# A graph network's last layer: edge features copied into step order during the dense pass, one load a group for the weighted pass, and its one-hot tiles shared by ACT and DVE

## The chip, the cores and the metric

One core of one Trainium2 chip. The metric is the device time of the whole program in microseconds, median of three runs. The engines are called PE (matrix products; PEld is its weight load), DVE (vector), ACT (scalar, pointwise functions), POOL (GpSimd) and SP (issues transfers only). The times of the program before are 5190.69 us (5190.12 to 5192.56).

## The reference

Four graph layers on 6250 nodes with 128 features, and 106250 edges sorted by destination. Only the last one is touched:

```python
xl = (x @ Wl + bl).reshape(n, HEADS, C)          # HEADS 4, C 32
xr = (x @ Wr + br).reshape(n, HEADS, C)
ee = (eattr @ We).reshape(-1, HEADS, C)          # eattr: 64 features of an edge, and for loops their mean by destination
msg = xl[src_a] + xr[dst_a] + ee
score = einsum('ehc,hc->eh', leaky_relu(msg, 0.2), att)
smax = segment_max(score, dst_a); ex = exp(score - smax[dst_a])
out = segment_sum(ex / segment_sum(ex)[dst_a] * xl[src_a], dst_a)
```

After it come a norm over the nodes, relu, and a layer norm of the sum with x. The third layer, which stands just ahead, is x + segment_sum(x[src], dst) and a layer norm.

## The kernel before, in words

Nodes stand in 49 tiles of 128. Edges stand in tiles of 128 in their sorted order, and a **step** is one pair of an edge tile and a node tile that its destinations touch. There are 896 steps (SPX), in 224 groups of GS = 4, and one turn of a hardware loop holds NG3 = 8 groups, so there are 28 turns; `turns` (L60) writes the first turn out apart and loops over 27. The table `g.t` holds the edge tile of each step, `g.T` its node tile; both are read into registers by a TENSOR_LOAD. The stages that matter here run one after the other, each in a block of its own that ends when all engines have come to its end.

**Dense pass** (`dense_pass`, L1982). Layer three is done with a dense matrix of edge counts in DRAM (`g.M`). SP loads it in chunks of four node tiles (`load`, L2007, 6.4 MB each, two buffers `matd`), the next chunk of a buffer as soon as PE has done the four tiles that read it (L2021). PE does 49 matmuls for each of the 49 tiles (L2033) into four PSUM banks. DVE adds the sums and does the layer norm (`add` L2070, `norm` L2082); ACT does one square root a tile (L2110) for which DVE waits in `norm`. The last chunk, number 12, has a single tile and is loaded when chunk 10 is done (L2023, L2024).

**Score pass** (`score_pass`, L2246), between the two stages that are changed. It loads the edge features transposed, one step at a time, by four transfers a group on SP (L2331), after a TENSOR_LOAD of the four tile numbers (L2327). It also gathers the rows of xl and keeps them in DRAM in step order (`g.rows`, L2314).

**Weighted pass** (`weighted_pass`, L2566). For each group G, with ring slot c = G mod 4:

- SP loads the four steps' rows of xl, one transfer (L2599). It waits for POOL to be through with group G-4 (`s_val`).
- ACT reads four tile numbers (L2629), waits until PE has done group G-4 (`s_o`, L2631), issues four transfers of edge features into the last 64 columns of `val` (L2633), and copies the weights of the steps into `val` (L2635).
- POOL multiplies rows by weights into `val` (L2616).
- DVE makes the one-hot tile `hot` of the destinations, 128 x 512 (L2675), and adds the products of group G-2 to the running sums `out` (`add`, L2660): a TENSOR_LOAD of four node tile numbers (L2661), and four adds of 128 x 200 (L2668), each waiting for the one before by `s_out`.
- PE multiplies `hot` and `val`, four steps a group (L2649; a matmul in f32 has two records each), into PSUM. There are two pairs of banks, so PE starts group G when the adds of group G-2 are done (`wait(t, s_out, (G - 1) * GS)`, L2647).

In its first turn SP also loads, after the rows of eight groups, xl and xr of all nodes (L2603, 3.2 MB each) and four vectors (L2606) for the stage that follows.

```python
    def add(G, q):
        v.load(regs, g.T[0:1, bass.ds(G * GS, GS)])
        T = [v.snap(r, min_val=0, max_val=NT - 1) for r in regs]
        wait(v, s_o, G + 1)
        for k in range(GS):
            wait(v, s_out, G * GS + k)
            to = g.out[:, bass.ds(T[k] * FX, FX)]
            v.tensor_tensor(to, to, ops[q % 2][k // 2][...], ALU.add).then_inc(s_out, 1)
```

## Time and profile before

| what | value |
|---|---|
| median of 3 runs | 5190.69 us |
| the profiled execution, its own time | 5189.41 us |
| its span (first to last instruction) | 5187.6 us |
| busy in the span: PE / DVE / ACT / POOL | 73% / 65% / 28% / 56% |
| dense pass | from about 2644 to 3070 us |
| score pass | from about 3117 to 4294 us |
| weighted pass | from about 4392 to 5036 us |

All positions are microseconds from the start of the span. Busy shares over the whole span say little here, since each stage has a bound of its own; the stages are read one by one. "Idle before" in a row is the time in which the engine had nothing to do just ahead of that instruction, with the event that ended it; "issue" means that no event of another engine ended it. Rows of DVEq, ACTq and SPq are work of the engines' instruction queues, such as a TENSOR_LOAD into registers or the issue of a transfer.

### The profile page before, as it was taken

Reading aid. Unit: us, or ns where it says so; the run is one execution under the profiler, and the core shown is the slowest. Engines: PE = TensorE matmul, PEld = TensorE weight load, DVE = VectorE, ACT = ScalarE, POOL = GpSimd, SP = SyncE. Lnnn points to the kernel's source line nnn. Section 1 sums busy time; section 2 is a strip of 40 time slices with the busy share of each in tenths; the row PEclk is TensorE's granted clock in tenths of the full one; section 3 lists DMA queues with packets and bytes.
Section 4 is the critical chain, followed back from the end, with each engine's and each line's share of the span. In section 5 each row is a group of like instructions: output and inputs, shape, how many; then the busy total and the mean of one; then the engine's idle time right before and its main releaser. Section 6 shows DMA issues by size and latency. Waiting matters only on the chain. (4 is left out here: it accounts for less than half of the span.)

```text
span 5187.6 us, 87634 instructions
## 1 busy us (share of the span) xinstructions
PE 3774.7 (73%) x17756; PEld 2581.4 (50%) x17757; DVE 3380.9 (65%) x10123; ACT 1428.3 (28%) x3423; POOL 2918.1 (56%) x2917
## 2 busy tenths in 40 slices
PE   0377777777677777389979988889899883555553
PEld 0266666666434444145546655555555552444442
DVE  5688888888798888343242234445444446788878
ACT  0255555555344434200000012222222221000012
POOL 1477777777367777777400007777777770333334
PEclk9955555665688888689989995555555555999996
DMA  5577777777532232088966636666666663655540
GB/s 104 154 249 250 248 247 248 247 249 254 164 97 87 87 92 91 10 183 199 180 182 205 204 113 171 177 174 179 174 176 177 175 168 59 174 143 142 143 106 25
DMA packets 1057791, 843.64 MB, mean 163 GB/s; under 512 B 546821, under 2 KB 952950, under 8 KB 1044160
## 3 DMA queue, kind: packets, MB, share of 16 engines
q1 hardware_dynamic: 785772, 597.52, 39.1%
q0 software_dynamic: 98096, 176.73, 13.3%
q10 hardware_dynamic: 173844, 68.53, 5.5%
q8 instruction: 26, 0.43, 0.0%
q14 instruction: 53, 0.43, 0.0%
HBM read 601.40 MB, written 167.28 MB: 148 GB/s over the span
## 5 line engine op out<-in xcount | busy, mean ns | idle before, releaser
L2303 POOL DMA_INDIRECT ring<-xl_rows,idx x896 | 895.2, 999 | 847.8 <-DVE idx L2382 575.0
L413 POOL DMA_INDIRECT ringa<-x_sign_pos,idxa x880 | 865.3, 983 | 301.6 <-issue 295.5
L965 POOL DMA_INDIRECT edge_counts<-edge_cnt,places x832 | 827.2, 994 | 359.9 <-issue 272.1
L2375 PE MATMUL zps<-We,eaT 64*128 64x128 f32 x1792 | 712.0, 499 | 0.0
L2649 PE MATMUL ops<-val,hot 128*128 128x200 f32 x1792 | 369.1, 350 | 273.5 <-DVE out L2668 243.1
L2373 PE MATMUL zps<-xr,hotT 128*128 x2688 | 455.2, 302 | 145.1 <-ACT hotT L2355 89.8
L2405 DVE TENSOR_TENSOR z<-zps,ring 128x512 f32<-128x512 f32 x224 | 154.9, 691 | 605.1 <-PE zps L2375 510.0
L2375 PEld LDWEIGHTS zps<-We,eaT 64*128 64x128 f32 x1792 | 448.6, 310 | 163.3 <-issue 145.7
L2616 POOL TENSOR_TENSOR val<-rows,val 128x512 f32<-128x512 f32 x224 | 235.0, 1050 | 508.4 <-ACT val L2635 377.6
L498 PE MATMUL sela<-hota,endsa 128*128 128x128 f32 x1760 | 399.3, 398 | 132.1 <-ACT endsa L439 117.6
L1890 PE MATMUL pss<-x3s,mats 128*128 128x385 bf16 x2401 | 403.4, 330 | 100.9 <-DMA mats<-edge_counts 95.9
L2649 PEld LDWEIGHTS ops<-val,hot 128*128 128x128 f32 x1792 | 301.2, 193 | 341.3 <-DVE out L2668 308.0
L2033 PE MATMUL psd<-x3d,matd 128*128 128x384 bf16 x2401 | 391.7, 327 | 35.3 <-DVE x3d L2064 35.3
L498 PEld LDWEIGHTS sela<-hota,endsa 128*128 128x128 f32 x1760 | 342.3, 290 | 149.9 <-issue 102.9
L2373 PEld LDWEIGHTS zps<-xr,hotT 128*128 128x128 bf16 x2688 | 225.3, 121 | 361.6 <-issue 354.9
L2351 ACT ACTIVATE apartT<-dstb,minus_p 128x512 f32<-128x512 f32 x224 | 161.7, 722 | 869.6 <-DMA dstb<-dst_in_tile 866.0
L2668 DVE TENSOR_TENSOR out<-out,ops 128x200 f32 x896 | 321.5, 359 | 115.5 <-PE ops L2649 17.6
L1890 PEld LDWEIGHTS pss<-x3s,mats 128*128 128x128 bf16 x2401 | 235.2, 98 | 269.2 <-DMA mats<-edge_counts 83.8
L1240 DVE SCALAR_TENSOR_TENSOR equalb<-keyb,key_cols,earlier 128x256 f32<-128x256 f32 x850 | 359.9, 481 | 5.9 <-issue 3.3
L506 PE MATMUL msgTa<-ident,msga 128*128 128x128 f32 x880 | 241.2, 428 | 153.3 <-DVE msga L578 150.8
L2033 PEld LDWEIGHTS psd<-x3d,matd 128*128 128x128 bf16 x2401 | 235.3, 98 | 191.7 <-DVE x3d L2064 35.7
L570 DVE TENSOR_TENSOR acc<-acc,sela 128x128 f32 x880 | 251.9, 286 | 117.5 <-issue 16.4
(359 smaller groups left out, 5945.3 us busy)
## 6 DMA issues: line engine op xcount, KB each, us to landing
edge_counts<-zeroa SPq DMA_DIRECT2D x55, 1568.0 KB
matd<-edge_counts SPq DMA_DIRECT2D x12, 6272.0 KB
keyb<-edge_keys SPq DMA_DIRECT2D x50, 1216.0 KB
dstb<-dst_in_tile SPq DMA_DIRECT2D x112, 512.0 KB
xl_of_steps<-ring SPq DMA_DIRECT2D x224, 256.0 KB
rows<-xl_of_steps SPq DMA_DIRECT2D x224, 256.0 KB
reseta<-resets SPq DMA_DIRECT2D x110, 512.0 KB
dstba<-dst_in_tile_bf ACTq DMA_DIRECT2D x112, 256.0 KB
```

The source lines that it names most:

```text
L413: p.indirect_dma_start(out=ring[:, k, :], out_offset=None, in_=table, in_offset=bass.IndirectOffsetOnAxis(ap=idx[:, k:k + 1], axis=0)).the ...
L498: ins = t.matmul(sel[q % 2][:, k * P:(k + 1) * P], ends[:, q % 2, k, :], hot[:, q, k, :], start=True, stop=True)
L570: v.tensor_tensor(to, to, sel[q % 2][:, k * P:(k + 1) * P], ALU.add).then_inc(s_acc, 1)
L965: p.indirect_dma_start(out=g.M.rearrange("d s -> (d s)").unsqueeze(1), out_offset=bass.IndirectOffsetOnAxis(ap=g.place[:, c:c + 1], axis=0 ...
L1240: v.scalar_tensor_tensor(out=equal[:, k % 4, :], in0=keyb[:, i, k * P + HALF:k * P + HALF + WIN], scalar=g.keycol[:, bass.ds(tile, 1)], in ...
L1890: ins = t.matmul(ps[b * WC + k][:, 0:3 * F + 1], mat[:, b, T, k * P:(k + 1) * P], x3[:, T, 0:3 * F + 1], start=T == 0, stop=T == NT - 1)
L2033: ins = t.matmul(ps[k][:, 0:3 * F], mat[:, b, T, k * P:(k + 1) * P], x3[:, T, :, :].rearrange("p i f -> p (i f)"), start=T == 0, stop=T == ...
L2303: p.indirect_dma_start(out=ring[:, c, k, :], out_offset=None, in_=g.xl_rows[0:N, :], in_offset=bass.IndirectOffsetOnAxis(ap=idx[:, q * GS ...
L2373: t.matmul(zk, hotT[:, b, k * P:(k + 1) * P], g.xr3[:, bass.ds(T[k] * (3 * F) + i * F, F)], start=i == 0, stop=False)
L2375: ins = t.matmul(zk, eaT[:, c, k, :], g.We[:, :], start=False, stop=True)
L2649: ins = t.matmul(ops[q % 2][k // 2][:, (k % 2) * FX:(k % 2 + 1) * FX], hot[:, c, k, :], val[:, c, k, :], start=True, stop=True)
L2668: v.tensor_tensor(to, to, ops[q % 2][k // 2][:, (k % 2) * FX:(k % 2 + 1) * FX], ALU.add).then_inc(s_out, 1)
```

## The change

In the dense pass, all 896 steps' edge features (32 KB each) are copied from the input in DRAM to a new tensor `g.ea` in DRAM, in step order. ACT issues eight copies ahead of each tile's square root (392), SP forty after each chunk's load and 24 at the end (504), each four after a TENSOR_LOAD of four tile numbers; SP waits for all of them at the end of the pass. In the weighted pass SP loads the edge features of a group by one transfer, behind the one for the rows and behind a wait for PE's group G-4. Of the eight one-hot tiles of a turn DVE makes numbers 3 and 7 (two groups ahead of need), ACT the six others, as 1 - |n - d| cut at zero: four Abs of 128 x 128, each with its step's destinations as bias, and one Relu of 128 x 512. DVE's adds now follow their own group's number instead of running two behind.

```diff
--- before.py
+++ after.py
@@ -1979,7 +1979,17 @@
                 norm(ch, CH * WC, 0)
 
 
-def dense_pass(nc, g):
+def copy_attributes(e, g, a, regs, at, n, sem):
+
+    for k in range(0, n, GS):
+        e.load(regs, g.t[0:1, bass.ds(at + k, GS)])
+        t = [e.snap(r, min_val=0, max_val=ET - 1) for r in regs]
+        for i in range(GS):
+            e.dma_start(g.ea[bass.ds(at + k + i, 1), :, :].rearrange("o p w -> o (p w)"),
+                        a["ea"][bass.ds(t[i], 1), :, :].rearrange("o p w -> o (p w)")).then_inc(sem, 16)
+
+
+def dense_pass(nc, g, a):
 
 
 
@@ -2001,9 +2011,18 @@
         tmp, z = m.sb("tmpd", [P, WC, F]), m.sb("zd", [P, WC, F])
         st, mv, root = m.sb("std", [P, WC, 6]), m.sb("mvd", [P, WC, 2]), m.sb("rootd", [P, WC])
         s_var, s_root, s_chain, s_go = m.sem("s_vard"), m.sem("s_rootd"), m.sem("s_chaind"), m.sem("s_god")
+        s_copied = m.sem("s_copied")
+        BY_TILE, BY_LOAD = 8, 40
+        REST = SPX - NT * BY_TILE - CH * BY_LOAD
+        assert 0 <= REST <= BY_LOAD and REST % GS == 0
         with nc.Block() as block:
             @block.sync
             def _(s):
+                regs = [s.alloc_register(f"tcs{j}") for j in range(GS)]
+
+                def copies(c, n=BY_LOAD):
+                    copy_attributes(s, g, a, regs, NT * BY_TILE + c * BY_LOAD, n, s_copied)
+
                 def load(c, b, w):
                     s.dma_start(mat[:, b, :, 0:w * P],
                                 g.M[0:NT * P, bass.ds(c * (WC * P), w * P)].rearrange("(t p) s -> p t s", p=P)
@@ -2016,12 +2035,17 @@
                         load(it * 2 + b, b, WC)
                 load(0, 0, WC)
                 load(1, 1, WC)
+                copies(0)
                 with s.Fori(1, PAIRS) as it:
                     for b in range(2):
                         s.wait_ge(s_pe, (it * 2 + b - 1) * WC)
                         load(it * 2 + b, b, WC)
+                        copies(it * 2 + b - 1)
                 s.wait_ge(s_pe, (CH - 1) * WC)
                 load(CH, 0, 1)
+                copies(CH - 1)
+                copies(CH, REST)
+                s.wait_ge(s_copied, 16 * SPX)
 
             @block.tensor
             def _(t):
@@ -2105,7 +2129,10 @@
 
             @block.scalar
             def _(e):
+                regs = [e.alloc_register(f"tca{j}") for j in range(GS)]
+
                 def one(S, i):
+                    copy_attributes(e, g, a, regs, S * BY_TILE, BY_TILE, s_copied)
                     e.wait_ge(s_var, S + 1)
                     e.activation(root[:, i:i + 1], mv[:, i, 1:2], ACT.Sqrt).then_inc(s_root, 1)
 
@@ -2577,8 +2604,20 @@
         ops = [[m.bank(f"ops4{i}{j}") for j in range(2)] for i in range(2)]
         s_ini = m.sem("s_ini4")
         s_r = [m.sem(f"s_r4{i}") for i in range(NG)]
+        apart = m.sb("apart4", [P, 2, GS * P])
         s_ea = [m.sem(f"s_ea4{i}") for i in range(NG)]
-        s_hot = m.sem("s_hot4")
+        s_ap = m.sem("s_ap4")
+        s_hot, s_hotd = m.sem("s_hot4"), m.sem("s_hotd4")
+        EQ = (3, 7)
+        assert NG3 == 8 and NG == 4
+
+        def on_act(it, q):
+
+            return it * (NG3 - len(EQ)) + q - sum(e < q for e in EQ)
+
+        def on_dve(it, q):
+
+            return it * len(EQ) + EQ.index(q)
         s_ex = m.sem("s_ex4")
         s_val = m.sem("s_val4")
         s_o = m.sem("s_o4")
@@ -2598,6 +2637,9 @@
                         wait(s, s_val, G - NG + 1)
                         s.dma_start(rows[:, c, :].rearrange("p (k f) -> p k f", k=GS),
                                     g.rows[bass.ds(G * GS, GS), :, :].rearrange("k e f -> e k f")).then_inc(s_r[c], 16)
+                        wait(s, s_o, G - NG + 1)
+                        s.dma_start(val[:, c, :, F + 2 * HEADS:FX],
+                                    g.ea[bass.ds(G * GS, GS), :, :].rearrange("k e f -> e k f")).then_inc(s_ea[c], 16)
                     if isinstance(it, int):
                         for to, of in ((g.xl, g.xl_rows), (g.xr, g.xr_rows)):
                             s.dma_start(to[:, :].rearrange("p (t f) -> p t f", f=F), of.rearrange("(t p) f -> p t f", p=P)
@@ -2621,19 +2663,24 @@
 
             @block.scalar
             def _(s):
-                regs = [s.alloc_register(f"t4{j}") for j in range(GS)]
-
                 def body(it):
                     for q in range(NG3):
                         G, c = it * NG3 + q, q % NG
-                        s.load(regs, g.t[0:1, bass.ds(G * GS, GS)])
-                        t = [s.snap(r, min_val=0, max_val=ET - 1) for r in regs]
                         wait(s, s_o, G - NG + 1)
-                        for k in range(GS):
-                            s.dma_start(val[:, c, k, F + 2 * HEADS:FX], a["ea"][bass.ds(t[k], 1), :, :].rearrange("o p w -> p (o w)")
-                                        ).then_inc(s_ea[c], 16)
                         s.activation(val[:, c, :, F:F + 2 * HEADS], exm[:, GS * q:GS * (q + 1), :, bass.ds(it, 1)].rearrange("p c k o -> p c (k o)"),
                                      ACT.Copy).then_inc(s_ex, 1)
+                        if q in EQ:
+                            continue
+                        A = on_act(it, q)
+                        b = on_act(0, q) % 2
+                        wait(s, s_hot, A - 1)
+                        for k in range(GS):
+                            ins = s.activation(apart[:, b, k * P:(k + 1) * P], g.iota_n[:, :], ACT.Abs, scale=-1.0,
+                                               bias=g.drel[:, bass.ds(G * GS + k, 1)])
+                        ins.then_inc(s_ap, 1)
+                        wait(s, s_ap, A + 1)
+                        s.activation(hot[:, c, :, :].rearrange("p k n -> p (k n)"), apart[:, b, :], ACT.Relu,
+                                     scale=-1.0, bias=1.0).then_inc(s_hot, 1)
                 turns(s, body, TURNS3)
 
             @block.tensor
@@ -2641,9 +2688,12 @@
                 def body(it):
                     for q in range(NG3):
                         G, c = it * NG3 + q, q % NG
-                        wait(t, s_hot, G + 1)
+                        if q in EQ:
+                            wait(t, s_hotd, on_dve(it, q) + 1)
+                        else:
+                            wait(t, s_hot, on_act(it, q) + 1)
                         wait(t, s_val, G + 1)
-                        t.wait_ge(s_ea[c], 64 * (slot(it, q) + 1))
+                        t.wait_ge(s_ea[c], 16 * (slot(it, q) + 1))
                         wait(t, s_out, (G - 1) * GS)
                         for k in range(GS):
                             ins = t.matmul(ops[q % 2][k // 2][:, (k % 2) * FX:(k % 2 + 1) * FX], hot[:, c, k, :],
@@ -2670,15 +2720,13 @@
 
                 def body(it):
                     for q in range(NG3):
-                        G, c = it * NG3 + q, q % NG
-                        wait(v, s_o, G - NG + 1)
-                        v.tensor_tensor(hot[:, c, :, :], bc_mid(g.iota_n[:, :], GS),
-                                        bc_last(g.drel[:, bass.ds(G * GS, GS)], P), ALU.is_equal).then_inc(s_hot, 1)
-                        if not (isinstance(it, int) and q < 2):
-                            add(G - 2, (q - 2) % NG)
+                        if q + 2 in EQ:
+                            G, c = it * NG3 + q + 2, (q + 2) % NG
+                            wait(v, s_o, G - NG + 1)
+                            v.tensor_tensor(hot[:, c, :, :], bc_mid(g.iota_n[:, :], GS),
+                                            bc_last(g.drel[:, bass.ds(G * GS, GS)], P), ALU.is_equal).then_inc(s_hotd, 1)
+                        add(it * NG3 + q, q % NG)
                 turns(v, body, TURNS3)
-                for b in (2, 1):
-                    add(TURNS3 * NG3 - b, NG - b)
 
 
 def node_tail(nc, g, a):
@@ -2993,6 +3041,7 @@
     g.xl_rows = dram("xl_rows", (NP, F))
     g.xr_rows = dram("xr_rows", (NP, F))
     g.rows = dram("xl_of_steps", (SPX, P, F))
+    g.ea = dram("edge_attr_of_steps", (SPX, P, DE))
     with ExitStack() as ctx:
         ctx.enter_context(nc.allow_non_contiguous_dma(reason="columns of positions and node tiles, a few thousand words"))
         m = Memory(nc, ctx)
@@ -3053,7 +3102,7 @@
                     first_layer(nc, g, a)
                     c0.close()
                     dense_sum(nc, g)
-        dense_pass(nc, g)
+        dense_pass(nc, g, a)
         layer3(nc, g, a)
```

**The adds and one-hot tiles on DVE, weighted pass, in the loop** (`out3` are the sums, `ops4ij` the four PSUM banks, `hot4` the one-hot tiles, ISA and REGISTER_ALU work on registers). Before, the piece from one group's last add to the next group's first:

```order
L2668 TENSOR_TENSOR out3<-out3,ops401 128x200
L2675 ISA
L2675 TENSOR_TENSOR hot4<-iota_n,drel 128x512
L2661 ISA
L2661 TENSOR_LOAD T
L2662 ISA
L2668 ISA
L2668 TENSOR_TENSOR out3<-out3,ops410 128x200
```

After, the same piece at six of the eight places of a turn:

```order
L2718 TENSOR_TENSOR out3<-out3,ops411 128x200
L2711 ISA
L2711 TENSOR_LOAD T
L2712 ISA
L2718 ISA
L2718 TENSOR_TENSOR out3<-out3,ops400 128x200
```

The one-hot tile that stood between the last add and the TENSOR_LOAD is gone there; at the other two places the piece reads as before.

**ACT, weighted pass, in the loop** (`val` the right-hand tiles, `exm` the weights, `in_ea` the input's edge features). Before, one group:

```order
L2629 TENSOR_LOAD t
L2630 ISA
L2633 ISA
L2633 DMA val<-in_ea 128x64
L2635 ISA
L2635 ACTIVATE val<-exm 128x4x8
```

After, one of the six groups with a one-hot tile:

```order
L2670 ISA
L2670 ACTIVATE val<-exm 128x4x8
L2678 ISA
L2678 ACTIVATE apart<-iota_n,drel 128x128
L57 REGISTER_ALU
L2682 ACTIVATE hot<-apart 128x512
```

Rows that only repeat are left out: the pair of L2633 stands four times in a group before, the pair of L2678 four times after. The transfers have left ACT, and five activations have come.

**ACT, dense pass, one tile** (`edge_attr_of_steps` is `g.ea`). Before, the loop held only the square roots:

```order
L2110 ACTIVATE rootd<-mvd 128x1
L2109 REGISTER_ALU
```

After:

```order
L1985 TENSOR_LOAD t
L1986 ISA
L1988 DMA edge_attr_of_steps<-in_ea 16x512
L1988 ISA
L2137 ACTIVATE rootd<-mvd 128x1
```

Ahead of each square root stand two TENSOR_LOADs and eight copies; each copy is written as 16 rows of 512 words. SP has the same rows behind each chunk's load.

## Rows read from the trace of the kernel before

**Rows 1.** Windows: length, busy time and count by engine, PEclk, DMA share, GB/s

```profile
4440.00:5036.00 596.00, 351.00 (x1728) 284.69 (x1728) 492.76 (x1077) 54.88 (x212) 224.54 (x215) 1.00 0.53 140
2676.00:3069.00 393.00, 390.85 (x2399) 234.86 (x2397) 97.62 (x390) 9.85 (x49) 0.00 (x0) 1.00 0.55 173
```

**Rows 2.** Waits, weighted pass: who for whom, us in total, times, longest

```profile
PE ops L2649 <- DVE out L2668: 243.1, 216, 1.6
...
DVE out L2668 <- PE ops L2649: 17.6, 4, 10.5
```

**Rows 3.** Timeline, weighted pass, two groups of the steady state: start, length

```profile
4620.99 1.86 DVE L2668 TENSOR_TENSOR out<-out,ops 128x200 f32 x4
...
4622.77 1.06 DVE L2675 TENSOR_TENSOR hot<-iota_n,drel 128x512 f32<-128x512 f32 x1
...
4622.91 1.62 PE L2649 MATMUL ops<-val,hot 128*128 128x200 f32 x8 [1.06 <-DVE out L2668]
4623.75 1.86 DVE L2668 TENSOR_TENSOR out<-out,ops 128x200 f32 x4
```

**Rows 4.** Timeline, weighted pass, over a turn's end

```profile
4631.75 1.86 DVE L2668 TENSOR_TENSOR out<-out,ops 128x200 f32 x4
...
4633.85 1.20 DVE L2675 TENSOR_TENSOR hot<-iota_n,drel 128x512 f32<-128x512 f32 x1 [0.23 <-issue]
4634.97 1.87 DVE L2668 TENSOR_TENSOR out<-out,ops 128x200 f32 x4
```

**Rows 5.** Lines by form, 4500 to 5000 us: count, busy, mean ns, idle

```profile
L2668 DVE TENSOR_TENSOR out<-out,ops 128x200 f32 x725 | 259.9, 359 | 77.7
```

**Rows 6.** Timeline, end of the weighted pass: three groups with no one-hot between

```profile
5029.46 1.86 DVE L2668 TENSOR_TENSOR out<-out,ops 128x200 f32 x4
...
5031.86 1.88 DVE L2668 TENSOR_TENSOR out<-out,ops 128x200 f32 x4 [0.54 <-DVE out L2668]
5034.13 1.88 DVE L2668 TENSOR_TENSOR out<-out,ops 128x200 f32 x4 [0.39 <-DVE out L2668]
```

**Rows 7.** Source lines L2661 and L2662: count, ns min/median/max

```profile
L2661 DVEq TENSOR_LOAD <-T x1: 350/350/350, 5033.4 to 5033.4; - x1
L2662 DVEq FUSED_REGOPS  x1: 120/120/120, 5033.8 to 5033.8; - x1
```

**Rows 8.** Timeline of ACT: activations of these shapes elsewhere in the kernel

```profile
1003.90 1.28 ACT L472 ACTIVATE sga<-ringa,zsa 128x128 f32<-128x128 f32 x4 [0.20 <-DVE zsa L618]
...
3600.49 0.63 ACT L2355 ACTIVATE hotT<-apartT 128x512 bf16<-128x512 f32 x1
...
4621.81 0.26 ACT L2635 ACTIVATE val<-exm 128x32 f32 x1 [2.42 <-issue]
```

**Rows 9.** Timeline, weighted pass, its first 50 us

```profile
4394.24 8.39 DVE L2656 MEMSET out<- 128x10000 f32 x1 [2.89 <-issue]
...
4404.87 0.84 SPq L2603 DMA_DIRECT2D xln<-xl_rows  x1
...
4438.39 2.05 POOL L2616 TENSOR_TENSOR val<-rows,val 128x512 f32<-128x512 f32 x2 [20.52 <-DMA rows<-xl_of_steps]
```

**Rows 10.** Windows of one chunk's load and of what follows, and of the saturated start

```profile
2740.70:2758.00 17.30, 17.30 (x109) 10.44 (x107) 4.99 (x21) 0.41 (x2) 0.00 (x0) 1.00 1.03 330
2758.00:2760.00 2.00, 2.00 (x14) 1.21 (x13) 0.82 (x4) 0.20 (x1) 0.00 (x0) 1.00 1.06 338
2760.00:2761.00 1.00, 1.00 (x8) 0.59 (x6) 0.00 (x0) 0.00 (x0) 0.00 (x0) 1.00 0.15 47
...
4403.00:4440.00 37.00, 18.15 (x65) 16.48 (x66) 18.61 (x43) 2.08 (x8) 7.06 (x7) 0.68 0.99 255
```

**Rows 11.** Timeline: four transfers issued in a row, on SP and on ACT

```profile
3606.18 2.46 SPq L2331 DMA_DIRECT2D eaT<-in_eaT  x4
...
4619.85 1.84 ACTq L2633 DMA_DIRECT2D val<-in_ea  x4
```

**Rows 12.** Source lines L2327 and L2599: register load and transfer issue on SP

```profile
L2327 SPq TENSOR_LOAD <-t x224: 294/314/840, 3117.0 to 4287.8; - x112
...
L2599 SPq DMA_DIRECT2D rows<-xl_of_steps x224: 367/373/1447, 4392.1 to 5018.5; - x112
```

**Rows 13.** Timeline of SP, dense pass: last chunk's load, and the next stage

```profile
3027.07 0.38 SPq L2008 DMA_DIRECT2D matd<-edge_counts  x1
3071.06 0.58 SPq L2947 DMA_DIRECT2D We<-in_L_gnn_We  x1
```

**Rows 14.** Waits, dense pass: who for whom, us in total, times, longest

```profile
ACT rootd L2110 <- DVE mvd L2080: 416.7, 49, 44.2
```

## The prediction

> **What bounds the kernel now.** I read the windows first, to have each touched stage apart, then the waits in each, then the timeline. In the weighted pass no engine is full: DVE is busy 493 of 596 us, PE 351 [rows 1]. The waits say who sets the pace: PE waits 243 us for DVE's adds, in 216 of 224 groups, and DVE's adds wait 18 us in all for PE, at the start alone [rows 2]. So DVE's chain of adds and one-hot tile is the bound, and its gaps belong to it. The timeline shows one group: four adds in 1.86 us (each 0.36 long, so 0.50 from start to start), then the one-hot tile, and the next adds 2.76 us after the first ones; PE needs 1.62 us of that [rows 3]. In 500 us of steady state there are 725 adds [rows 5], that is 181.25 groups, 2.76 us each and **22.07 us a turn of eight**. The group at a turn's end is the long one, 3.22 us from adds to adds [rows 4], so the seven others average 2.69.
>
> In the dense pass PE is busy 390.9 of 393 us [rows 1]; it is the bound, and transfers hide under it. A chunk of four tiles takes PE 31.9 us (390.9 / 49 x 4). Its 6.4 MB load runs from 2740.7 to about 2760.2, 19.5 us at 330 GB/s, and after it the transfer engines stand still [rows 10]: 12.4 us are free in each chunk.
>
> **The weighted pass, where the gain is.** DVE keeps two one-hot tiles of eight. It would be easy to take off six times their 1.06 us, but the tile also covers something: a TENSOR_LOAD of the node tile numbers (0.35) and the register work behind it (0.12) stand ahead of the first add [rows 7] and run while the one-hot tile does. The added order rows show that at six places a turn this load now follows the last add with nothing to cover it. The trace has this very case: the last groups of the pass have no one-hot tile between them. There DVE stood idle 0.54 and 0.39 us, and adds followed adds after 2.40 and 2.27 us [rows 6], against 2.69. So an exported tile brings 0.29 to 0.42 us, not 1. Inside the loop an address has to be computed ahead of the load, which is not so in the last group; the first of the two also has the loop's exit in it. I take 2.35. The two groups with a tile stay at 2.69. At a turn's end before, DVE sat idle 0.23 us where the tile normally starts 0.08 before the adds end, and the tile was longer [rows 4]: 0.53 in all, of which 0.31 is the queue's. Without a tile I take 0.40 on top of 2.35. A turn is then 5 x 2.35 + 2 x 2.69 + 2.75 = **19.88 us**, 2.19 less than 22.07. For the 27 turns behind the first: **-59 us**. With 2.27 and 0.31 it is -75, with 2.40 and 0.53 it is -48.
>
> Is anything else late next? PE is let go by adds two groups back, so its 1.62 us stand beside 2.35 or more of adds; 0.7 us to spare. POOL's product is 1.03 us (two in 2.05 [rows 9]). ACT now makes six tiles a turn: four activations of 128 x 128 take 1.28 us together, one of 128 x 512 takes 0.63, the weights' copy 0.26 [rows 8]; with 0.1 for the wait between, 2.3 us, and six of them and two lone copies 14.3 us a turn against DVE's 19.88. ACT also runs up to four groups ahead, so three such groups in a row drain nothing. Its four transfers (1.84 us [rows 11]) and TENSOR_LOAD are gone. SP's second transfer a group waits for PE's group G-4 and holds back the rows of G+1; both are 0.37 us to issue [rows 12], and PE comes to group G some 8 us after it is through with G-4, so I count zero.
>
> **The start of the weighted pass: +4 us.** Before, SP could issue the loads of xl and xr at 4404.87, and the rows of group 8 landed behind them at 4438.39, with POOL idle 20.5 us [rows 9]. The transfer engines are full there, 0.99 at 255 GB/s [rows 10], so that end moves with the loads. Now the edge features of group 7 stand ahead of them in SP's queue, waiting for PE's group 3. That one needs the adds of group 1, which cannot start before the memset ends at 4402.6: two groups of adds, then 1.6 to 2.4 us of PE, about 4409. Bounds: +2 and +6.
>
> **The copies in the dense pass.** ACT issues eight a tile. At its own row (four in 1.84) and 0.4 for each register load (0.31 on SP [rows 12], and 0.12 to unpack [rows 7]) that is 4.5 us, in a tile of 8.0 us of which ACT waits nearly all, 416.7 us for 49 tiles [rows 11, 14]: zero, and if it were late by more than 3.5 us, DVE's norm would be late and then PE's bank. SP issues forty a chunk. The nearest row by path is 0.37 us a transfer plus about 0.15 of register work [rows 12], the dearest 2.46 for four [rows 11]; with a register load of 0.31 and 0.2 for the unpacking and addresses behind it, four copies cost 2.6 to 3.2 us and forty 26 to 32, against 31.9. A small excess is absorbed, since a load has 12.4 us of slack. It is not absorbed at the end: the last load is issued at 3027.07 and then come 64 copies, 42 to 51 us, so SP is done at 3069 to 3078 plus some 2 us of landing, and the next stage's transfer was issued at 3071.06 [rows 13]. I take **+5 us**, bounds 0 and +11.
>
> The transfers themselves: 72 copies of 32 KB a chunk. No row shows a copy from DRAM to DRAM of this shape. By bytes at 330 GB/s one costs 0.099 us, at the 255 GB/s of small rows 0.129 [rows 10]; if reading and writing DRAM both count in full, twice that, 0.257. The 12.4 free us hold 72 copies up to 0.172 us each. The copies are 16 rows of 2 KB, larger than the 1 KB and 0.5 KB rows behind these rates, so I take the first two (7 to 9 us of the 12.4), which cost nothing. The Trainium skill speaks against this edit (DMA: Bandwidth & Descriptors, Bandwidth): transfers under 64 KB are dominated by descriptors, with 64 KB at 0.95 us. By that rate an estimate is 0.24 us a copy, 17 us a chunk, 4.7 us more than there is room for, and the sum would come out near no change. Those are single loads, where here transfers queue behind one another; no row of this trace settles it.
>
> **Sum.** 5189.4 (the profiled execution, 1.3 below the median of 5190.7) - 59 + 4 + 5 = **5139 us**. From the bounds: 5189.4 - 75 + 2 + 0 = 5116 to 5189.4 - 48 + 6 + 11 = 5158.
>
> **The rivals.** *The register load is hidden after all* (13%): if the queue gets to it early, adds follow adds at 0.50 us across groups as within one, and a group is 2.00 us. A turn is 10.0 + 5.4 + 2.3 = 17.7, the gain 118, the time 5189.4 - 118 + 9 = 5080. Rows 6 speak against it.
>
> *The copies are dearer than their bytes* (7%), the case that ends slower. At 0.257 us a copy, 72 take 18.5 us; with the load's 19.5 that is 38.0 for a chunk of 31.9. Each load lands 6.1 us late and PE waits for it, some 11 times: +67, so 5139 + 67 = 5206. It outweighs the gain from 0.235 us a copy. For it: reads and writes meet in DRAM. Against it: the rows of these copies are larger than any behind the rates of rows 10. The skill's rule above is this mechanism at 0.24 us.
>
> *ACT becomes the bound* (5%): it takes 3.2 us for a group with a tile instead of 2.3. At 3.5 a turn is 21.6, the gain 13, the time 5185. Against it are rows 8, where such activations follow one another every 0.30 us.
>
> *The copies' issue on SP is slower than any row* (3%), say 4.0 us for four: forty take 40 us, the slack is used up and the pass grows by over 60 us; about 5200.
>
> **How the numbers follow.** The forecast's own case has 72%, 5116 to 5158. The range takes the hidden load in and leaves the last three out: 5080 to 5160. A measurement of this kernel tells about 0.2% (10 us) from no change. Faster: 0.72 + 0.13 and a part of the ACT case, 0.88; within 0.2%: 0.05; slower: 0.07.
>
> **What would show it.** DVE's first add of a group without a tile has 0.4 to 0.5 us idle ahead, and groups are 2.35 us apart; ACT's 128 x 128 activations in fours take about 1.3 us; PE in the dense pass has no wait for `matd`; SP's last copy is issued at about 3073, and the score pass starts 5 us later and lasts as before. The forecast is wrong if PE waits for `hot` from ACT or for `matd`, or if adds of neighbouring groups run at 0.50 us.

## The result, and the profile after

| | before | the change |
|---|---|---|
| median, us | 5191.62 (5190.12 to 5201.15, 4 runs) | 5379.2 (5377.4 to 5389.32, 4 runs) |
| dense pass, first load of `matd` to the next stage's load of `We` | 426.7 | 671.3 |
| PE's last matmul of it, from the same start | 422.1 | 629.8 |
| from that load of `We` to the weighted pass's memset | 1323.1 | 1325.3 |
| weighted pass, memset to the next stage | 642.6 | 580.7 |

The change is **slower**: 1.0355 times the time before, 95% interval 1.0339 to 1.0371. The forecast was 5139 us, the range 5080 to 5160, with a chance of 0.07 for slower. The table takes the profiled executions apart by stage: the weighted pass won 62 us and the dense pass lost 245.

From the profile's page of the changed kernel, the granted clock in 40 slices and the dense pass's matmuls:

```profile
PEclk9856555555788888699897877555555555699996
...
L2057 PE MATMUL psd<-x3d,matd 128*128 128x384 bf16 x2401 | 418.0, 340 | 216.7 <-DMA matd<-edge_counts 181.4
```

**The dense pass.** Its waits (who waits for whom, us in all, times, longest), where before PE was busy 390.85 of 393 us [rows 1]:

```profile
PE psd L2057 <- DMA matd<-edge_counts: 181.4, 10, 22.1
```

PE stood ten times for its chunk, up to 22 us. Who made the chunks late is in the timeline of SP (start, length, queue, line, transfer, count), 2700 to 2830 us:

```profile
2713.43 0.41 SPq L2027 DMA_DIRECT2D matd<-edge_counts  x1
2714.90 52.15 SPq L1988 DMA_DIRECT2D edge_attr_of_steps<-in_ea  x40
2767.34 0.40 SPq L2027 DMA_DIRECT2D matd<-edge_counts  x1
2768.75 52.79 SPq L1988 DMA_DIRECT2D edge_attr_of_steps<-in_ea  x40
2824.83 0.40 SPq L2027 DMA_DIRECT2D matd<-edge_counts  x1
2826.17 13.60 SPq L1988 DMA_DIRECT2D edge_attr_of_steps<-in_ea  x1
```

A chunk's forty copies take SP 50 to 53 us, PE's work on a chunk 31.9 us; the next chunk's load stands in the same queue behind them. The last row is the new thing: **one** copy, the first behind a chunk's load, was in issue for 13.6 us. I call this its stand. The source line of the copies, 2765 to 2790 us (count, ns min/median/max), gives both prices, 0.52 us as a rule and 15.3 us once:

```profile
L1988 SPq DMA_DIRECT2D edge_attr_of_steps<-in_ea x10: 520/521/15286, 2765.0 to 2789.3; - x10
```

With the register load and the address work, four copies in the loop took 3.87 us, 0.97 us each: 13.6 + 39 x 0.97 = 51.4, where that chunk's forty took 50.4. Were the transfers full meanwhile? The windows (length, busy time of PE, PEld, DVE, ACT, POOL with counts, PEclk, DMA share, GB/s), during a load, during the copies behind it, while PE stood, and after it had begun again at 2790.6:

```profile
2720.00:2730.00 10.00, 10.00 (x63) 6.06 (x62) 2.86 (x11) 0.20 (x1) 0.00 (x0) 1.00 1.09 364
2740.00:2750.00 10.00, 10.00 (x63) 6.05 (x62) 2.00 (x8) 0.20 (x1) 0.00 (x0) 1.00 0.28 65
...
2780.00:2790.00 10.00, 0.00 (x0) 0.00 (x0) 0.00 (x0) 0.00 (x0) 0.00 (x0) 0.50 1.01 338
...
2794.00:2798.00 4.00, 4.00 (x18) 2.06 (x17) 0.00 (x0) 0.00 (x0) 0.00 (x0) 0.68 0.17 38
2798.00:2802.00 4.00, 4.00 (x27) 2.38 (x26) 0.19 (x1) 0.00 (x0) 0.00 (x0) 1.00 0.13 33
```

They were at 0.28 while forty copies were issued, so it was SP's issue that was full. Second price: in the window in which PE stands its granted clock is 0.50, 1.2 in place of 2.4 GHz, and when it begins again the clock is not back at once: 18 matmuls in 4 us at 0.68, then 27 at 1.00. PE's busy time in the pass is 418.0 us, against 390.85 before [rows 1]. Third: at the end SP still had 64 copies behind the last load.

```profile
3253.58 0.41 SPq L2027 DMA_DIRECT2D matd<-edge_counts  x1
3254.64 61.37 SPq L1988 DMA_DIRECT2D edge_attr_of_steps<-in_ea  x64
3318.73 0.53 SPq L2995 DMA_DIRECT2D We<-in_L_gnn_We  x1
```

Their source line, 3262 to 3318 us, shows a stand of 10.5 us here too:

```profile
L1988 SPq DMA_DIRECT2D edge_attr_of_steps<-in_ea x64: 512/513/10458, 3254.6 to 3315.5; - x64
```

PE ended at 629.8 and the next stage began at 671.3, 41.5 us later (4.6 before). So the 245 us are some 181 of PE's waits, 27 of slower matmuls and 37 at the end.

**The weighted pass.** DVE's timeline over one turn's end; in brackets the idle time before:

```profile
4900.38 1.88 DVE L2718 TENSOR_TENSOR out<-out,ops 128x200 f32 x4 [0.50 <-DVE out L2718]
4902.18 0.68 DVE L2726 TENSOR_TENSOR hot<-iota_n,drel 128x512 f32<-128x512 f32 x1
4902.93 1.87 DVE L2718 TENSOR_TENSOR out<-out,ops 128x200 f32 x4
...
4907.64 1.88 DVE L2718 TENSOR_TENSOR out<-out,ops 128x200 f32 x4 [0.48 <-DVE out L2718]
4910.40 1.87 DVE L2718 TENSOR_TENSOR out<-out,ops 128x200 f32 x4 [0.88 <-DVE out L2718]
```

Groups without a one-hot are 2.34 to 2.37 us apart, as at the end of the pass before [rows 6]; with one 2.55 (2.69 before), across a turn's end 2.76 (3.22 [rows 4]). In 500 us DVE makes 814 adds, where before they were 725 [rows 5]:

```profile
L2718 DVE TENSOR_TENSOR out<-out,ops 128x200 f32 x814 | 294.5, 362 | 174.5 <-DVE out L2718 84.0
```

That is 2.457 us a group, **19.66 us a turn**.

### The profile page after: what moved, and what is told of

It reads as the page before. It is cut to its first block and busy times, and to the rows that moved or that the text cites. A ratio compares the mean times of both kernels' runs of the same rounds, so it can differ in the third digit from the quotient of the medians.

```text
span 5378.0 us, 90473 instructions
## 1 busy us (share of the span) xinstructions
PE 3801.3 (71%) x17756; PEld 2583.6 (48%) x17757; DVE 3226.4 (60%) x9955; ACT 1732.1 (32%) x4263; POOL 2928.3 (54%) x2917
## 5 line engine op out<-in xcount | busy, mean ns | idle before, releaser
L2057 PE MATMUL psd<-x3d,matd 128*128 128x384 bf16 x2401 | 418.0, 340 | 216.7 <-DMA matd<-edge_counts 181.4
```

Of the source, the lines that this page charges most:

```text
L2057: ins = t.matmul(ps[k][:, 0:3 * F], mat[:, b, T, k * P:(k + 1) * P], x3[:, T, :, :].rearrange("p i f -> p (i f)"), start=T == 0, stop=T == ...
```

## The experiments

They ran on other chips, where the kernel before takes 6549 to 6584 us (medians) and runs of one kernel lie up to 0.8% apart. The added time lies ahead of the dense pass, which begins 3679 to 3709 us into the program in place of 2644, and in the score stage; both have indirect transfers. Where a kernel leaves the dense or the weighted pass as in one of the two kernels above, that pass comes out as above to within 2 us, so the table goes by stage (all in us), and the ratios are to the kernel before on the same chip.

| run | us | ratio [95%] | dense | PE's last matmul | score stage | weighted |
|---|---|---|---|---|---|---|
| quarter bytes | 6746.2 | 1.026 [1.023, 1.0289] | 663.2 | 622.3 | 1642.7 | 581.1 |
| pairs | 6513.1 | 0.9905 [0.9876, 0.9934] | 427.9 | 423.3 | 1646.5 | 580.9 |
| sixteen | 6528.7 | 0.9924 [0.9886, 0.9962] | 427.7 | 423.2 | 1662.6 | 582.7 |
| twenty-four | 6557.5 | 0.996 [0.9939, 0.9981] | 471.1 | 465.2 | 1653.2 | 581.8 |
| half loads | 6508.2 | one run | 426.6 | 422.1 | 1651.7 | 581.5 |
| copies on POOL | 6509.7 | 0.9892 [0.9864, 0.9921] | 427.2 | 423.1 | 1656.8 | 581.6 |
| copies in the score pass | 6623.7 | 1.0067 [1.0046, 1.0088] | 428.1 | 423.6 | 1778.7 | 580.1 |
| loads only | 6607.5 | 1.0038 [1.0018, 1.0059] | 427.0 | 422.5 | 1651.5 | 675.0 |
| product behind one-hot | 6555.4 | 1.0009 [0.9993, 1.0024] | 428.2 | 423.7 | 1639.6 | 649.9 |
| the same, loads only | 6516.2 | one run | 427.5 | 423.0 | 1635.7 | 609.1 |
| no copies | 6708.4 | one run | 426.9 | 422.3 | 1661.4 | 762.7 |
| POOL, tiles ahead | 6492.5 | 0.9864 [0.9836, 0.9893] | 427.3 | 423.2 | 1642.5 | 562.0 |
| all one-hots on ACT | 6494.0 | 0.9865 [0.9834, 0.9895] | 426.4 | 422.3 | 1649.2 | 556.8 |

### Is it the bytes or the issue? Quarter bytes, and pairs

```diff
-            e.dma_start(g.ea[bass.ds(at + k + i, 1), :, :].rearrange("o p w -> o (p w)"),
-                        a["ea"][bass.ds(t[i], 1), :, :].rearrange("o p w -> o (p w)")).then_inc(sem, 16)
+            e.dma_start(g.ea[bass.ds(at + k + i, 1), 0:P // 4, :].rearrange("o p w -> o (p w)"),
+                        a["ea"][bass.ds(t[i], 1), 0:P // 4, :].rearrange("o p w -> o (p w)")).then_inc(sem, 16)
```

(The weighted pass then reads edge features at fixed places of the input.) 

> Each of the 896 copies moves a quarter of its bytes (8 KB), with as many transfers issued as in the change; the weighted pass reads its edge features from the first 32 tiles of the input instead, with transfers of the same shape. Theory A (SP's instruction queue is the bound: it stands about 14 us behind each chunk's load and then takes 0.97 us a copy, 52 us a chunk): bytes do not matter, about 5375 us, SP's copies still 50 to 53 us a chunk, PE still waits some 180 us for matd. Theory B (the copies' transfers fill the engines or DRAM): the copies cost a quarter, the dense pass goes back to about 393 us, the program to about 5131 us.

The dense pass stayed at 663 us with a quarter of the bytes. SP's timeline:

```profile
4199.24 0.40 SPq L2027 DMA_DIRECT2D matd<-edge_counts  x1
4200.56 52.78 SPq L1988 DMA_DIRECT2D edge_attr_of_steps<-in_ea  x40
4253.63 0.38 SPq L2027 DMA_DIRECT2D matd<-edge_counts  x1
4255.03 13.01 SPq L1988 DMA_DIRECT2D edge_attr_of_steps<-in_ea  x1
```

The same 52.8 us for copies of 8 KB as for 32 KB, and stands of 16.1 and 13.0 us in the chunks shown, where in the loop of the change they are 13.3 to 15.8: SP does not pay by bytes. (The copies are still 16 rows each; a price by rows of a copy is not told apart from one by issue.) In the next run SP issues one transfer of 64 KB for two copies (from places next to each other, so the step order is not kept):

```diff
+            if odd is None:
...
+            elif i % 2 == 0:
+                e.dma_start(g.ea[bass.ds(at + k + i, 2), :, :].rearrange("o p w -> (o p) w"),
+                            a["ea"][bass.ds(odd + k + i, 2), :, :].rearrange("o p w -> (o p) w")).then_inc(sem, 32)
```

> SP issues one copy of 64 KB in place of two of 32 KB (source tiles in plain order, so the features are another step's); same bytes in all, half as many transfers from SP. Theory A: a chunk is 0.4 + 14 + ten blocks of about 2.5 us = 39 us of SP, against 31.9 of PE: PE loses some 7 us a chunk less 12 us of slack, the program is at about 5195 us. Theory B: same bytes, same time, about 5379 us.

```profile
4021.97 0.39 SPq L2031 DMA_DIRECT2D matd<-edge_counts  x1
4022.70 30.74 SPq L1992 DMA_DIRECT2D edge_attr_of_steps<-in_ea  x20
4053.74 0.38 SPq L2031 DMA_DIRECT2D matd<-edge_counts  x1
```

All bytes moved, half of SP's issues, and the dense pass was back at 428 us, better than I had expected. The expectation had 2.5 us for each block of four tiles, 39 us a chunk; behind a stand of 14.4 us the blocks took some 1.7, and SP's 31.1 us fitted in PE's 31.9.

### How large are the two prices? Sixteen and twenty-four copies a chunk

Only the number of SP's copies is changed; the others are left out.

```diff
-                        copies(it * 2 + b - 1)
+                        copies(it * 2 + b - 1, 16)
```

> SP issues 16 copies a chunk instead of 40 and none at the end, ACT all of its own; the rest is left out (the weighted pass reads the first 32 tiles of the input). Theory A: 0.4 + 14 + four blocks of 3.87 us = 30 us of SP a chunk, just under PE's 31.9, so the dense pass is as before the change and the program at about 5131 us. Theory B (cost in proportion to bytes): 48 of 72 copies are left, so a part of the 248 us stays, 5200 us or more.

> As with sixteen, but 24 copies a chunk from SP. Theory A: 0.4 + 14 + six blocks of 3.87 = 37.6 us a chunk, 5.7 more than PE needs; over eleven chunks less 12 us of slack PE loses about 50 us: 5180 us. If the 14 us behind the load were not SP's to bear (theory A without the stand), 24 copies would be 23.6 us and cost nothing: 5131 us.

Sixteen took 27.5 us and PE never waited for `matd`. Twenty-four, in SP's timeline:

```profile
4072.40 0.39 SPq L2027 DMA_DIRECT2D matd<-edge_counts  x1
4073.85 34.92 SPq L1988 DMA_DIRECT2D edge_attr_of_steps<-in_ea  x24
4109.06 0.38 SPq L2027 DMA_DIRECT2D matd<-edge_counts  x1
```

36.7 us from load to load, a dense pass of 471 us. Stand plus 0.97 us a copy comes within 1 us of what was measured at 24 and at 40 (35.8 for 34.9, 51.4 for 50.4).

### What the stand is: half loads

Twenty-four copies again, but the chunk's load in two halves with twelve copies behind each:

```diff
-                        load(it * 2 + b, b, WC)
-                        copies(it * 2 + b - 1, 24)
+                        half(it * 2 + b, b, WC, 0, 25)
+                        copy_attributes(s, g, a, regs, NT * BY_TILE + (it * 2 + b - 1) * BY_LOAD, 12, s_copied)
+                        half(it * 2 + b, b, WC, 25, NT)
+                        copy_attributes(s, g, a, regs, NT * BY_TILE + (it * 2 + b - 1) * BY_LOAD + 12, 12, s_copied)
```

> Of the dense pass alone. The kernel with 24 SP copies a chunk (dense pass 471 us, 36.6 us a chunk), but the chunk load is issued in two halves of 3,200 and 3,072 rows, with 12 copies behind each. Edge features are as in that run not all copied. First theory: SP's queue takes a bounded number of rows, and what is issued behind a load stands until the load's last rows are taken in. 6,272 rows move in some 20 us and the stand is 14 us, so rows worth some 6 us fit; a half moves in 10 us and would make the next one stand 4 us. A chunk then costs SP 24 x 0.97 + 2 x 0.4 + 2 x 4 = 32 us against PE's 31.9: dense pass 427 to 440 us. Rival one: the stand is a fixed price of a large load, 14 us each: 23.3 + 0.8 + 28 = 52 us a chunk, dense pass about 670 us. Rival two: the stand is in proportion to the load, 7 us each: it stays at 37 to 38 us a chunk, dense pass 471 to 490 us.

```profile
3981.24 0.38 SPq L2027 DMA_DIRECT2D matd<-edge_counts  x1
3982.65 14.15 SPq L1988 DMA_DIRECT2D edge_attr_of_steps<-in_ea  x12
3997.00 0.43 SPq L2027 DMA_DIRECT2D matd<-edge_counts  x1
```

Twelve copies take 14.15 us, 2.5 more than 12 x 0.97, where a fixed stand would make them 25 and one in proportion nearly 19. The longest single copy between 4040 and 4062 us is 3.9 us (over the loop these stands are 3.5 to 4.6):

```profile
L1988 SPq DMA_DIRECT2D edge_attr_of_steps<-in_ea x18: 520/521/3910, 4039.7 to 4061.4; - x18
```

The same 24 copies now cost nothing (426.6 us, not 471), with the same bytes moved. The longest stand of the run, 8.3 us, was at its start, behind four half loads in a row.

This is what the first theory of the expectation forecasts: a queue with bounded room, in which the next transfer stands until the load's last part is taken in. Is the room counted in bytes or in rows? The last load of the pass tells. It has a single node tile, so its 6,272 rows are 256 B each and its 1.6 MB a quarter of a chunk's. Of a chunk's 19.5 us some 5 to 6 are left when the stand ends; at 330 GB/s that is room for 1.65 to 2 MB (an estimate), and the whole last load would fit. Yet the copy behind it stood 10.5 us in the change and 8.2 to 9.4 us in four of the kernels of the table (copies on POOL, sixteen, twenty-four, pairs). So the stand goes with the rows of the load rather than with its bytes. What exactly is full, these runs don't show.

### Another engine's queue: copies on POOL, and in the score pass

POOL is idle in the dense pass. It issues 312 of the 896 copies there, SP 16 a chunk, ACT 8 a tile as in the change. Nothing is left out.

```diff
-        BY_TILE, BY_LOAD = 8, 40
+        BY_TILE, BY_LOAD = 8, 16
...
+            @block.gpsimd
+            def _(p):
+                regs = [p.alloc_register(f"tcp{j}") for j in range(GS)]
+                copy_attributes(p, g, a, regs, NT * BY_TILE + CH * BY_LOAD, REST, s_pool)
+                p.wait_ge(s_pool, 16 * REST)
```

> All 896 copies stay in the dense pass, but SP has only 16 a chunk, and POOL, idle there, issues the other 312. Theory A (SP's instruction queue was the bound): SP takes 28 us a chunk, the dense pass is at 427 us as before the change, and the weighted pass keeps its 581: about 62 us faster than before, ratio 0.988. Theory B (the engines or DRAM are filled by the copies): the bytes are those of the change, and 300 us of POOL's copies lie beside the loads, so PE waits again and the dense pass is longer by tens of us.

```profile
L1988 POOL DMA_DIRECT2D edge_attr_of_steps<-in_ea x312: 486/486/578, 3690.3 to 3918.5; - x156
```

POOL was through in 229 us, 0.73 us a copy, none over 0.58 in issue; no chunk load stands in its queue. All 896 copies were made and the dense pass took 427.2 us. This is the change's gain without its loss. It also tests the transfers harder than the change did: while POOL copies, some 90 copies go beside each chunk. From 3785 to 3913 us PE was busy for all 128 us, with a DMA share of 0.92. There is little to spare: SP's sixteen copies took 31.2 us here, not 27.5. In the next version ACT makes 336 copies in the dense pass and 560 in the score pass, five groups of eight getting four copies each, SP none.

```diff
+                        if q < 5:
+                            copy_attributes(s, g, a, regs, 6 * 56 + it * 20 + q * 4, 4, s_copy)
```

> SP issues no copy. ACT issues 336 in the dense pass (eight ahead of seven of eight square roots) and 560 in the score pass, four behind each of five of eight one-hot tiles. ACT there works 1.35 of 5.2 us a group, and four copies take some 3.3 us. If ACT's tiles are not late by it: dense pass 427 us, score pass as before, weighted 581, ratio 0.988. If ACT's one-hot tiles are late, PE waits in the score pass by up to 1 us in such a group, 140 us in all: ratio 1.01.

The score stage grew by some 125 us, near the 140 of the expectation's second case. Between 4700 and 5600 us, where both kernels are in the score pass, ACT's idle time ahead of its next tile that no event of another engine ended is 287 us, where it is 104 with the copies on POOL, and DVE's waits that the view puts down to `remote` are 470 us against 404. So the copies in ACT's queue make its tiles late, though ACT is busy for under a fifth of the stage. By which step its lateness reaches the end of the stage is not shown.

### What made the weighted pass faster: the loads, or the shared one-hots?

SP loads a group's edge features in one transfer, ACT issues none, all one-hots stay on DVE, and nothing is copied (the features come from fixed places of the input):

```diff
+                        wait(s, s_o, G - NG + 1)
+                        s.dma_start(val[:, c, :, F + 2 * HEADS:FX],
+                                    a["ea"][bass.ds(q * GS, GS), :, :].rearrange("k e f -> e k f")).then_inc(s_ea[c], 16)
...
-                        for k in range(GS):
-                            s.dma_start(val[:, c, k, F + 2 * HEADS:FX], a["ea"][bass.ds(t[k], 1), :, :].rearrange("o p w -> p (o w)")
-                                        ).then_inc(s_ea[c], 16)
```

> The kernel before with only the loads of the weighted pass changed: SP loads the edge features of a group in one transfer (from the first 32 tiles of the input, so another step's), ACT issues none; DVE makes all one-hot tiles and runs its adds two groups behind, and there are no copies. Theory C (the 62 us gained in the weighted pass come from the six one-hot tiles taken off DVE): ACT's transfers hid under DVE, so the pass stays at 643 us, the ratio to before is 1.000. Theory D (they come from the four transfers a group taken off ACT): the pass is at about 581 us, the ratio 0.988.

It became **slower** by 32 us, which I had not foreseen. Its DVE line from 5850 to 6350 us, with 1139 ns for the one-hot, where before the mean was 1019:

```profile
L2671 DVE TENSOR_TENSOR hot<-iota_n,drel 128x512 f32<-128x512 f32 x173 | 197.0, 1139 | 4.9 <-issue 4.9
```

224 x 0.12 is 27 of the 32 us. And its timeline shows what stands beside a long one-hot and what beside a short one:

```profile
6003.40 1.05 POOL L2619 TENSOR_TENSOR val<-rows,val 128x512 f32<-128x512 f32 x1 [2.24 <-DMA rows<-xl_of_steps]
6003.42 1.58 DVE L2671 TENSOR_TENSOR hot<-iota_n,drel 128x512 f32<-128x512 f32 x1
...
6014.53 1.05 POOL L2619 TENSOR_TENSOR val<-rows,val 128x512 f32<-128x512 f32 x1 [1.43 <-ACT val L2631]
...
6015.36 0.77 DVE L2671 TENSOR_TENSOR hot<-iota_n,drel 128x512 f32<-128x512 f32 x1
```

Wholly beside POOL's product it takes 1.58 us, nearly free of it 0.77. Two more runs are to take the overlap away, by one wait in POOL's loop, in the kernel before and in the loads-only kernel:

```diff
+                        wait(p, s_hot, G + 1)
                         p.tensor_tensor(val[:, c, :, 0:F].rearrange("p k (h c) -> p k h c", c=C),
```

> The kernel before with one wait more: POOL's product of a group starts only when DVE's one-hot of that group is done, so the two never run at the same time. First theory: the one-hot is stretched by POOL's product beside it (0.68 us at best, 1.02 on the mean before, 1.14 with one load a group). It then takes 0.68 each time, and a group's pitch is the 2.55 us of the change's groups with a one-hot: a turn of 8 x 2.55 + 0.63 = 21.0 us in place of 22.07, 28 turns, 29 us less: weighted pass 614 us (643 before), dense pass as before. Rival: the one-hot's length comes from something else, such as the loads it runs beside: it stays near 1.0 us and the pass at 643 us, or longer, as the product comes later in each group.

> The same wait in the kernel in which SP loads each group's edge features in one transfer and ACT issues none (weighted pass 675 us, 32 more than before; edge features come from fixed places, so the output is not the reference's). First theory: the 32 us are 224 one-hots at 1.14 in place of 1.02 us (27 us), because POOL's product, no longer behind ACT's late coefficients, lies wholly beside the one-hot. With the wait the pass comes to 614 us too, 61 less. Rival: SP's load or its place is what costs 32 us: 640 to 650 us.

In the loads-only kernel it did: DVE's line, 5900 to 6300 us, and a stretch of the timeline.

```profile
L2672 DVE TENSOR_TENSOR hot<-iota_n,drel 128x512 f32<-128x512 f32 x155 | 106.2, 685 | 4.7 <-issue 4.7
```

```profile
6102.34 0.69 DVE L2672 TENSOR_TENSOR hot<-iota_n,drel 128x512 f32<-128x512 f32 x1
...
6103.04 1.88 DVE L2665 TENSOR_TENSOR out<-out,ops 128x200 f32 x4
6103.20 1.05 POOL L2620 TENSOR_TENSOR val<-rows,val 128x512 f32<-128x512 f32 x1 [1.48 <-DVE hot L2672]
```

The pass fell from 675.0 to 609.1 us, by a wait alone. (The one-hots are shorter by 224 x 0.45 = 101 us; where the other 35 went is not shown.) In the kernel before, the run missed: 649.9 us, one-hot still 0.97 in the median. POOL waits there for ACT's copy of the weights, which stands behind four transfers in ACT's queue, so the product runs beside the **next** group's one-hot, which this wait does not hold off:

```profile
6104.64 1.05 POOL L2617 TENSOR_TENSOR val<-rows,val 128x512 f32<-128x512 f32 x1 [1.64 <-ACT val L2636]
6105.01 1.83 ACTq L2634 DMA_DIRECT2D val<-in_ea  x4
6105.25 0.98 DVE L2676 TENSOR_TENSOR hot<-iota_n,drel 128x512 f32<-128x512 f32 x1
```

The product's last 0.44 us lie beside the one-hot here. That run therefore tests nothing about the stretching; its edit did not take the overlap away.

### Are the copies needed? No copies

One-hots shared as in the change, but SP loads a group's features in four transfers by the table, straight from the input.

```diff
+                        s.load(regs, g.t[0:1, bass.ds(G * GS, GS)])
+                        t = [s.snap(r, min_val=0, max_val=ET - 1) for r in regs]
+                        for k in range(GS):
+                            s.dma_start(val[:, c, k, F + 2 * HEADS:FX], a["ea"][bass.ds(t[k], 1), :, :].rearrange("o p w -> p (o w)")
+                                        ).then_inc(s_ea[c], 16)
```

> The kernel before in its dense pass, no copies at all; in the weighted pass the one-hots are shared as in the change, and SP in place of ACT loads a group's edge features in four transfers by the table's tile numbers. If what the copies buy is that one transfer takes the place of four, SP is now the bound: a register load 0.35 + 0.16, four issues 1.84, the row load 0.38: 2.73 us a group against DVE's 2.46, 224 groups and 30 us of ends: 640 us, no better than the kernel before (643). Rival: freeing ACT is all, and SP's work hides under DVE's: 581 us, with the dense pass at 427, so that the whole would be faster than before by some 60 us without any copy.

It was worse than both theories: 762.7 us, not 640, some 3.3 us a group. SP is the bound, with next to no gap between its work:

```profile
6199.85 1.88 SPq L2629 DMA_DIRECT2D val<-in_ea  x4
...
6201.94 0.38 SPq L2623 DMA_DIRECT2D rows<-xl_of_steps  x1
...
6203.02 1.88 SPq L2629 DMA_DIRECT2D val<-in_ea  x4
```

Between row load and feature loads there are 0.70 us for register load and addresses, where I had counted 0.51, and 0.21 us ahead of the row load, which I had not counted: 3.17 us from group to group here, not 2.73. So the copies do buy something: one issue a group in place of four and a register load.

### Versions that beat both: node tile numbers ahead, and all one-hots on ACT

To the version with copies on POOL comes this: DVE loads the next group's node tile numbers behind its first add and unpacks them behind its second.

```diff
+                        if k == 1 and place < NG3 - 1:
+                            load_tiles(G + 1, place + 1)
+                        if k == 2 and place < NG3 - 1:
+                            unpack(place + 1)
```

> As b1, and in the weighted pass DVE reads the next group's four node tile numbers behind the first add of a group instead of ahead of its own first add (two sets of registers; at a turn's start as before). Theory E (the 0.48 us that DVE stands idle ahead of a group without a one-hot tile is the register load): it is gone at five of eight places, a turn is 2.0 us shorter, the weighted pass about 525 us, the ratio to before 0.977. Theory F (the idle is the wait for PE or for the sums): no change against b1, 0.988.

```profile
6009.29 0.36 DVE L2736 TENSOR_TENSOR out<-out,ops 128x200 f32 x1 [0.21 <-DVE out L2736]
6009.97 1.37 DVE L2736 TENSOR_TENSOR out<-out,ops 128x200 f32 x3 [0.32 <-DVE out L2736]
6011.56 0.36 DVE L2736 TENSOR_TENSOR out<-out,ops 128x200 f32 x1 [0.21 <-DVE out L2736]
```

The idle time ahead of the first add fell from 0.48 to 0.21, and 0.32 came up ahead of the second: the load moved, and little of it was hidden at these places (2.27 us a group, 2.36 before). The larger part of the gain lies at the groups with a one-hot: the group behind it now has its load under the one-hot and takes 2.08 us, not 2.35. In all the weighted pass is 20 us shorter, not 56. Then all eight one-hots go to ACT (`EQ = ()`):

> The version with copies on POOL and with node tile numbers loaded ahead (dense pass 427, weighted pass 562 us), with all eight one-hots of a turn on ACT, none on DVE. If DVE's adds bound the weighted pass, its two groups a turn with a one-hot (0.68 + 1.87 + 0.1 = 2.65 us) come down to the others' pitch of 2.28: 0.74 us a turn, 28 turns, 21 us: weighted pass 541 us. ACT then has 8 x (0.26 + 1.27 + 0.63) = 17.3 us of work in a turn of 18.3. Rival: ACT bounds, since it starts a group only when PE has freed its block and has gaps of 0.1 to 0.5 us in each: 8 x 2.4 = 19.2 us a turn, weighted pass 565 us or more.

Weighted pass 556.8 us, 5 less, not 21. ACT keeps up (between 5900 and 6440 us PE waits for DVE's adds alone), but the 0.68 us of DVE had covered the next group's register load, which now stands bare there too. Both versions take less time than the kernel before, 0.9864 and 0.9865 of it; that is under 2%, but the intervals leave 1 out. Between the two, and against copies on POOL alone (0.9892), the whole program tells no difference for certain; by their stages they are the fastest kernels of this study.

## Why the prediction was wrong, point by point

**The step that failed is the price of the forty copies on SP**, put as "four copies cost 2.6 to 3.2 us and forty 26 to 32, against 31.9". Measured: 52 us. Two things were missing. A copy cost 0.97 us in the loop, not 0.65 to 0.8, because issuing it takes 0.52 us (I had taken the 0.37 of another shape of transfer [rows 12] as the nearest row) and the register and address work makes up the rest. And the first one behind a chunk's load stood some 14 us, a term that the prediction does not have. By the first alone forty would be 39 us and the pass longer by some 80 us (an estimate); the stand is the larger part. (The prediction's own rows give 2.97 for its dearer bound, 2.46 + 0.31 + 0.2, not 3.2.) The trace of before had rows for the stand: the source line of the chunk's load, and, at the start of the weighted pass, the first small transfer behind the loads of xl and xr.

```profile
L2008 SPq DMA_DIRECT2D matd<-edge_counts x13: 378/382/13848, 2644.4 to 3027.1; - x13
...
4416.68 13.57 SPq L2606 DMA_DIRECT2D vbias_out<-in_L_gnn_bias_out  x1
```

The loads were issued in 0.38 us as a rule and one took 13.8: the second, the only one right behind another. The prediction says nothing of either row. In all these traces a transfer that SP issues right behind such a load stands, whatever its size, and the change put one behind every chunk.

**The transfers themselves**: right. 72 copies a chunk, and some 90 for a while, cost nothing that can be measured (427.2 us with all 896 copies made). The rival that the copies are dearer than their bytes got the sign of the result but not its cause; a quarter of the bytes gave the same time. The Trainium skill (DMA: Bandwidth & Descriptors, Bandwidth) counts 64 KB at 0.95 us; the estimate of 4.7 us too much a chunk that I drew from it does not show in any run here.

**SP's issue slower than any row** (3%) was the right rival, at 4.0 us for four and "about 5200". Four took 3.87 us, but its time, too, lacked the stand, and what a wait of PE costs beyond its length: 27 us of matmuls at the lower clock level.

**The end of the dense pass**, +5: +37. 64 copies took 61.4 us, not 42 to 51: 10.5 us of it are the stand, and the other 63, outside the loop, took 0.81 us each, 51 in all, the top of what I had. The rest is the late start: the last load was itself issued late, 23.6 us ahead of PE's end, where before it was 39.4. (The bound of +11 is 2 more than its own terms give.)

**ACT's eight copies a tile at zero**: right, but with less room than I had. They took 6.5 us, not 4.5, in a tile of 8.0.

**The weighted pass**: 19.66 us a turn against 19.88, and the pass with its start 62 us shorter against 59 - 4 = 55. By term: 5 x 2.35 is 5 x 2.36; the turn's end 2.75 is 2.76; the two groups with a one-hot, 2.69, are 2.55, since POOL's product is no longer beside the one-hot (0.683 us in place of 1.02). That makes up most of the difference (0.22 x 27 = 6 of 7 us). The start, +4: the load of `xl` was issued 17.4 us behind the memset's start, 10.6 before, 6.8 us later, but POOL's product of group 8 began only 1.5 us later (45.7 us behind the memset's start, 44.2 before), so that end did not move with the loads as I had it; why is not shown. In all the pass lost some 3 us to its ends (27 x 2.41 = 65, less 62), within my +2 to +6: the size was right, the way to it not. ACT's tiles came out as summed (1.28, 0.63 and 0.26 us), and PE's weight loads waited for them 1.1 us in all. That the register load stays bare was right, and the rival of a hidden one wrong; an attempt to hide it got 20 us of 56. Why the pass gained was only half seen. Against 643 us before, the product out of the one-hot's way gives 609 (with the loads on SP), sharing the one-hots 581 (the first with all of them on DVE, so these are two steps of one way, not two parts of the change).

## What to carry to other kernels

Before work is put on a queue that looks idle, price the transfers in it by their own issue time and look for the longest issue of each line, not the median: behind a load of 6,272 rows the next transfer stood 8 to 16 us here, and everything behind it, the next load too, was late. If a load must share its queue, split it (24 copies behind one load cost 44 us, behind two halves nothing) or give the small transfers to an engine that issues no large ones. And an instruction much longer than its fastest instance is a place to look: here one wait on POOL, which kept its product off DVE's one-hot, was worth 66 us of 675, and left the pass 34 us under that of the kernel before.

## What the runs showed of the hardware that I had not expected

- A transfer on SP right behind one load of 6,272 rows of 1 KB stood 13 to 16 us in issue, whether it moved 6.4 MB, 32 KB or 8 KB; behind 6,272 rows of 256 B, 8 to 10.5 us; behind half a load (3,200 or 3,072 rows of 1 KB), 3.5 to 4.6 us.
- Issue of a DRAM to DRAM copy took 0.52 us on SP, 0.53 on ACT, 0.49 on POOL; with register load and addresses 0.97 in SP's loop and 0.81 outside it, 0.82 on ACT and 0.73 on POOL.
- The comparison of 128 x 512 on DVE took 0.68 us alone and up to 1.58 us beside a product of POOL's of 128 x 512 that had begun first; POOL's then stayed at 1.05 us. Where DVE's had begun first it was the other way round: in the change, at 4912 us, the comparison kept its 0.68 us and POOL's product, begun 0.30 us into it, took 1.28.
- While PE stood in the dense pass (2780 to 2790 us) its granted clock was 0.50; over the pass it was 0.81.
